# Later places for the attention matmuls in the last scan row, and an index load placed behind the last repeated row of C

## The reference

```python
x = _layernorm(x + _L0_attn_ref(x, weight_qkv, weight_proj))
x = _layernorm(x + _L0_xattn_ref(ctx, x, ...))     # scan, gated by silu(x)
x = _layernorm(x + _L0_ffn_ref(x, lut, gate_idx, up_idx, down_idx))
...
def step(state, xs):                               # 512 positions, 512 channels, 16 states
    dA = jnp.exp(d_t[..., None] * A)
    state = state * dA + (d_t * u_t)[..., None] * B_t[:, None, :]
    y_t = jnp.einsum('ben,bn->be', state, C_t)
```

## Time and profile before

| what | value |
|---|---|
| median of 3 runs | 990.57 us (990.4 to 994.05) |
| profiled execution, its own time | 990.59 us |
| span of the profile | 988.8 us |
| PE busy | 869.3 us (88%) |
| DVE busy | 765.2 us (77%) |
| ACT busy | 672.4 us (68%) |
| POOL busy | 481.3 us (49%) |
| mean granted TensorE clock | 0.906 of full speed |

### The profile page before, as it was taken

The page is one execution under the profiler, slowest core; times in us unless marked ns, Lnnn a source line. Parts: engine busy times, 40 slices in busy tenths (PEclk is TensorE's granted clock), DMA queues, the critical chain, the costliest instruction groups (busy, mean ns, idle before and its releaser), DMA issues.

```text
span 988.8 us, 11890 instructions
## 1 busy us (share of the span) xinstructions
PE 869.3 (88%) x3824; PEld 626.4 (63%) x3824; DVE 765.2 (77%) x1066; ACT 672.4 (68%) x994; POOL 481.3 (49%) x445
## 2 busy tenths in 40 slices
PE   6879888787878897787989879899999999899997
PEld 3547654465544674456545457787777778688885
DVE  3797899877998879986788666888888888355442
ACT  4698985789956899668696464777777776242321
POOL 0079867799767998669676631221112111001000
PEclk9789777999779797787979988999999999899998
DMA  8167979589996799967999222111111110223221
GB/s 259 39 168 177 209 161 229 117 221 245 210 224 122 204 241 210 224 125 202 208 289 277 83 96 86 46 61 42 42 42 44 62 42 22 75 86 107 86 64 53
DMA packets 49908, 135.99 MB, mean 138 GB/s; under 512 B 5364, under 2 KB 13684, under 8 KB 41156
## 3 DMA queue, kind: packets, MB, share of 16 engines
q0 software_dynamic: 8064, 58.72, 30.9%
q1 hardware_dynamic: 40432, 76.44, 23.1%
q10 hardware_dynamic: 1364, 0.25, 0.2%
HBM read 57.93 MB, written 78.51 MB: 138 GB/s over the span
## 4 chain that ended last, share of the span: by engine, by line
PE 26%; issue 23%; DVE 23%; ACT 19%; POOL 5%; DMA 4%; DVEq 1%; ACTq 0%; POOLq 0%; SPq 0%
DVE state L1191 6%; PE banks L606 5%; ACT decay L893 5%; PE banks L720 5%; ACT scaled L882 5%; PE banks L744 4%; DVE leaf L1219 3%; DVE w_gu L1219 3%; PE banks L644 3%; PE banks L548 3%; DVE conv_in L1094 3%; POOL state L1442 2%; ACT leaf L1001 2%; DMA hT<-y_scratch 2%; DMA y_scratch<-state 1%
## 5 line engine op out<-in xcount | busy, mean ns | idle before, releaser
L1442 POOL TENSOR_TENSOR state<-state,crep 128x512 f32<-128x512 f32 x243 | 334.8, 1603 | 85.9 <-DVE state L1191 79.7
L1191 DVE TENSOR_TENSOR_SCAN state<-decay,banks 128x512 f32<-128x512 f32 x243 | 280.7, 1202 | 54.2 <-PE banks L644 44.6
L720 PE MATMUL banks<-x2T,wgu 128*128 128x512 f32 x1056 | 246.3, 393 | 4.8 <-DVE hT L1270 4.1
L644 PE MATMUL banks<-ident,scaled 128*128 128x128 f32 x1024 | 175.9, 314 | 69.1 <-DVE state L1191 49.7
L720 PEld LDWEIGHTS banks<-x2T,wgu 128*128 128x128 f32 x1056 | 197.9, 189 | 52.1 <-DVE hT L1270 11.3
L644 PEld LDWEIGHTS banks<-ident,scaled 128*128 128x128 f32 x1024 | 136.2, 161 | 143.1 <-DVE state L1191 63.4
L893 ACT ACTIVATE decay<-delta,negA 128x512 f32<-128x512 f32 x256 | 169.9, 722 | 77.6 <-DVE state L1191 69.8
L882 ACT ACTIVATE scaled<-duT,BT 128x512 f32<-128x512 f32 x256 | 163.8, 720 | 0.0
L1001 ACT ACTIVATE leaf<-idx_sb,table,table_gap 128x1024 f32<-128x1024 uint8 (+1 forms) x132 | 129.4, 1022 | 6.8 <-DVE w_down L1219 3.2
L1219 DVE COPY_PREDICATED leaf<-idx_sb,leaf 128x1024 f32<-128x1024 uint8 (+1 forms) x88 | 94.1, 1069 | 7.1 <-issue 6.1
L1534 POOL TENSOR_TENSOR pool_wait_here<-minus_half 128x1 f32<-128x1 f32 x22 | 4.3, 193 | 180.6 <-DVE w_gu L1219 116.2
(11 more groups left out here) (140 smaller groups left out, 1155.6 us busy)
## 6 DMA issues: line engine op xcount, KB each, us to landing
y_scratch<-state POOLq DMA_DIRECT2D x52, 1024.0 KB, 8.5
crep<-c_scratch SPq DMA_DIRECT2D x64, 256.0 KB, 5.4
idx_sb<-in_idx SPq DMA_DIRECT2D x11, 512.0 KB, 3.5
xT_sb<-in_xT SPq DMA_DIRECT2D x16, 256.0 KB, 4.8
y_scratch<-u SPq DMA_DIRECT2D x4, 1024.0 KB, 6.1
y_scratch<-state SPq DMA_DIRECT2D x4, 1024.0 KB, 6.3
leaf<-x_scratch SPq DMA_DIRECT2D x16, 256.0 KB, 2.8
out<-leaf SPq DMA_DIRECT2D x16, 256.0 KB, 2.0
```

Of the source, the lines that this page charges most:

```text
L644: last = nc.tensor.transpose(banks[:, k % NB, lc * LQ:(lc + 1) * LQ], scaled[:, g % SR, lc, et * P:(et + 1) * P], ident[:])
L720: last = mm(banks[:, 2 * tb + w, :], wgu[par][:, w, ws, t * P:(t + 1) * P], x2T[:, tb, xs, t, :], start=t == 0 and n == 0, stop=t == HT - ...
L1191: V.tensor_tensor_scan(state[:, g % GR, et, :], decay[:, k % DR_RING, :], banks[:, k % NB, :], 0.0, ALU.mult, ALU.add).then_inc(scan_ready, 1)
L1442: G.tensor_tensor(state[:, g % GR, et, :], state[:, g % GR, et, :], crep[:, g % CR, :], ALU.mult)\
```

## The change

All in the last row, except where the SP queue is named. No instruction is added or removed.

```diff
-        LAST_ATT_AT = {(3, 0): 3, (3, 1): 0, (4, 0): 2, (5, 0): 1}
+        LAST_ATT_AT = {(3, 3): 3, (4, 0): 0, (4, 2): 2, (6, 1): 1}
...
-        LAST_PROJ_AT = {(5, 1): 3, (5, 3): 2, (6, 1): 1, (6, 3): 0}
+        LAST_PROJ_AT = {(5, 1): 3, (5, 3): 2, (7, 0): 1, (7, 2): 0}
...
-                        if b == S - 1 and n == 11:
+                        if b == S - 1 and n == 13:
                             sp.dma_start(table[:], lut.to_broadcast([P, 16])).then_inc(lut_in, 16)
...
-                        if n == 2:
+                        if n == (2 if more else 3):
                             keep_attT(b, 3)
                             keep_attT(b, 0)
-                        elif n == (4 if more else 3):
+                        elif n == 4:
                             keep_attT(b, 2)
-                        elif n == (5 if more else 4):
+                        elif n == (5 if more else 6):
                             keep_attT(b, 1)
-                        if n == 8 and not more:
+                        if n == 9 and not more:
                             normalized(b)
...
-                LAST_RES_AT = {(5, 2): 3, (6, 0): 2, (6, 2): 1, (7, 0): 0}
+                LAST_RES_AT = {(5, 2): 3, (6, 0): 2, (7, 1): 1, (7, 3): 0}
...
-                            if at == ((15, 2) if more else (7, 1)):
+                            if at == ((15, 2) if more else (8, 1)):
                                 norm_factors(b)
```

## The result

The changed kernel takes 994.89 us (median of 20 runs, 992.29 to 999.2), the kernel before 991.38 us on the same chips (20 runs, 988.04 to 994.8). The ratio is 1.0035, with a 95% interval of 1.0023 to 1.0047: slower by 3.5 us, 2.3 to 4.7. The forecast was 991.9 against 990.59, +1.3 us, in a range of 986 to 996.

The account below looks back on a forecast made before the run. The prediction took the work queued on the DMA engines, which sets when row 3 of `y_scratch` lands, as the bound. It summed 990.59 - 1.3 (DMA gap) + 2.6 (TensorE's clock) = 991.9 us, range 986.0 to 996.0.

Parts of the forecast that it names:

- What bounds the kernel: Before the feed-forward block: row 3 lands when the DMA queues' work is done, at 101% of the engines; earlier issue alone won't help.
- rival 2: The queue gives way: row 3, issued 5 us earlier, lands 5.6 earlier; 985.0 to 987.6 us, chance 0.15.
- Scan (8, 0) starts at about 493.0: Walk through the last row's attention jobs: this scan starts at 493.0 instead of 495.11, about 2 us of stalls gained.
- ring of projection 1, copy and decay: At (7, 0): projection 1 waits about 4.6 us for att 1's copy behind state 8's decays, then takes 5.4 us.
- rival 3: Slower: projection 1's wait 5 us longer, (8, 0) at 498, row 0 issued 6 us later; 996 to 998 us, chance 0.15.
- (8, 0) after 495: Sign in the profile that the forecast is wrong and rival 3 came: scan (8, 0) starting later than 495 us.
- -1.3: DMA term: the gap of idle engines from 492 to 496 us closes, so the same bytes end 1.3 us earlier.
- price of one us for each us of (8, 0): In rival 3: from (8, 0) later than about 495, each us costs one, +3 to +5 us.
- +2.6: Clock term: TensorE, idle 7 to 14 us before `rest_summed`, restarts at half clock and loses 2.6 us.
- Hidden: 0: Index loads behind the last `crep`: indices land at 541 at the latest, VectorE wants them about 538; cost 0.
- price of one us for each us of bits after 549: Without cover for the index loads, GpSimd's `gate_row(1)` waits for the bits; each us after about 549 costs one.
- The norm a state later: Factors come near 499.2 and row 0 goes out 1.2 us later, at about 499.3; row 0 loses nothing by it.

Follow-up runs that it names:

- e8: Changed kernel with the addition of odd states to loaded row 2 left out but for 128 of 2048 columns: 990.27 us, 0.9982 of the kernel before.
- e5: e2 with projections 1 and 0, their residuals and the norm's factors moved earlier: 989.17 us, 0.9965 of the kernel before.
- e2: Changed kernel with ScalarE's copy of att 1 behind the decays of state 7 (n = 5), not state 8: 988.16 us, 0.9948 of the kernel before.
- e4: Kernel before with the norm alone moved: factors behind (8, 1), normalising at n = 9: 994.31 us, 1.0018.
- e3: Kernel before with the index loads alone moved from n = 11 to n = 13: 993.88 us, 1.0011.
- e6: e2 with att 3, 0 and 2 and their copies back at their places of before: 987.28 us, 0.9949 of the kernel before.
- e10: Kernel before with the edits of e3 and e4 together, all attention jobs as before: 992.03 us, 0.9994.
- e1: Changed kernel with the index loads back at n = 11: 998.22 us, 1.0058 of the kernel before.

## Why the prediction was right, and where not

- **What bounds the kernel: right, and shown.** The work of the DMA engines sets when row 3 lands. e8 takes 0.94 MB of additions out and wins 4.6 us at an unchanged request; at 5.75 MB in 52.2% of 53 us an addition of 1 MB costs 4.8. e5 asks for row 0 4.7 us earlier and wins nothing. Not settled is whether an earlier request for row 3 alone would bring it earlier: in e2 it goes out at +91.9 instead of +96.5 and lands 4.1 us earlier, near what rival 2 had for a queue that gives way, and request and bytes moved together there.
- **"Scan (8, 0) starts at about 493.0": the step that failed.** The ring of projection 1, copy and decay was named in the walk and in rival 3, but mis-sized. The wait came out at 6.21 us against 4.6, the projection at half clock at 6.45 against 5.4. And the walk left out two waits for additions, at (4, 0) and (6, 0): 4.40 and 2.97 us. I had let (4, 0) start 3.4 us earlier than before; it starts at +26.85 against +26.84. The result is +3.1 us instead of -2.1. e2 undoes the ring with one number, (8, 0) comes 7.1 us earlier, and the time is 8.6 us lower by the ratios. By the prediction's own signs ("(8, 0) after 495") it is rival 3 that came, to which it gave 0.15: on the scale of the trace before, (8, 0) is at 498.2 for its 498, and row 0 goes out 6.8 us later for its 6.
- **"-1.3", the gap in the DMA share: wrong sign, by that step.** With factors 8.5 us later in the row and row 0 asked for 6.8 later, the engines were idle 2.4 us more in 20 and 2.1 more up to the landing, and `rest_summed` started 2.2 us later. The rule behind the term (idle time closed or opened is the time won or lost) held here; in e2 it gives 1.5 of 4.1 us, since the bytes also took less of the engines. e4 has the late norm without the late (8, 0), with row 0 asked for 3.8 later, and opens no idle time, so it takes the ring to open it. Rival 3's price of one us for each us of (8, 0) was too high; of 3.1 us 2.2 came through.
- **"+2.6", the clock: right in kind in the trace, 1.5 there** (5.22 against 3.70), 2.1 in e3, 2.6 in e6, 2.7 in e10 (6.44 us). Its weight in the median is not settled: e6 and e2 take the same time within their intervals, though e6's trace restarts at half clock (6.31 us) and e2's does not (3.70). Either the other executions of e6 restart at full clock, or another difference covers it; no run tells. The places in single traces are no better a measure of the time elsewhere: at L1251 e4's trace is 4.5 us behind that of before where 1.8 was measured, e6's 1.3 ahead where 5.1 was.
- **"Hidden: 0", the index loads: right by itself** (e3: 1.0011, and the interval includes 1), but perhaps not in the changed kernel: there they save 2.3 us by the ratios (e1 1.0058 against 1.0035, intervals of 1.0040 to 1.0076 and 1.0023 to 1.0047) and 5.4 at the start of `rest_summed`. With the factors late, `load_row` and the additions crowd the queues later, and the cover of the last repeated row, 1.7 us in the kernel before, is used up. The bits came at +118.2 instead of +115.7 and cost nothing: VectorE had to wait for the indices until +115.0 and +116.3, 548.5 and 549.9 on the scale of the trace before, where I had "541 at the latest", and GpSimd was still through with `gate_row(2)` at +128.7, before L1251. So the price of one us for each us of bits after 549 was wrong too.
- **The norm a state later**: I costed 1.2 us of delay as covered. e10 against before (0.9994) bears that out with the index move; e4 (1.0018) without it, where the repeated row of C came 9.26 us late, suggests that it needs that move.

So the sum was -1.3 + 2.6 = +1.3, and it is +2.2 + 1.5 = +3.7. The direction was right by luck in good part: the first term had the wrong sign, and the second, which carried the forecast, is seen in the trace but settled by no median. That 3.7 stands so near the measured 3.5 is partly luck too.

The version to keep is that of e2 or e6, att 1 behind (6, 1) with its copy at n = 5: 0.9948 and 0.9949.

## What to carry to other kernels

When a job moves to a later place on one engine, move its consumer's place on the next engine only as far as the data needs, and look up what stands in front of it there: behind a decay that waits for a scan that waits for the job's own engine, one place too late closed a ring, with a wait of 6.2 us in it. Where the DMA engines are full, count the bytes and the idle time up to the landing that is waited for, before you price an earlier request. A wait that is hidden has a cover of a certain length: write it down beside the wait (here 1.7 us), because the next change may use it up.

## What was not expected of the hardware

GpSimd's additions take most of the engines while both queues hold work. In the stretch of the earlier trace rows, where SP's queue has 16.2% of the engines, GpSimd's queue stands so:

```profile
q0 software_dynamic: 414, 3.13, 88.3%
```

A repeated row of C of 256 KB landed 8.5 to 12.9 us after GpSimd had wanted it (e2, e1). That was seen before, if smaller (6.09 us); not expected was that the same 16 MB take the engines 57 us in some versions and 55 in others (before and e2, e6).
